# Four batches through an attention, FFN, quaternion attention and expert chain: later turns, spreading in four steps, later loads, and score matmuls in pairs of half the rows

## Time and profile before

| what | us |
|---|---|
| median of 3 runs | 871.47 (870.83 to 872.36) |
| the profiled execution | 872.1 |
| its span | 869.9 |
| TensorE busy in the span | 736.0 (85%) |
| ScalarE busy | 501.3 (58%) |
| VectorE busy | 419.1 (48%) |
| GpSimd busy | 180.4 (21%) |

### The profile page before, as it was taken

One profiled execution on the slowest core, in us unless ns is written; L12 is line 12 of the kernel. 1 busy time (PEld: TensorE's weight loads), 2 busy tenths in 40 slices (PEclk: granted clock), 3 DMA queues, 4 the chain that ended last, 5 costly groups with the idle time before them and its releaser, 6 DMA issues. The chain is left out here.

```text
span 869.9 us, 21028 instructions
## 1 busy us (share of the span) xinstructions
PE 736.0 (85%) x8160; PEld 522.1 (60%) x8160; DVE 419.1 (48%) x1389; ACT 501.3 (58%) x1030; POOL 180.4 (21%) x307
## 2 busy tenths in 40 slices
PE   4779997989779999888989987887786878789994
PEld 3668775768545667665555753455553656467763
DVE  3355426664253464225353566473866646531236
ACT  3456564586557586866658765558454556543231
POOL 7101010000100000010100005132315287036230
PEclk9999998999889999999999999999887999989997
DMA  4610400002400000511000412000511021101010
GB/s 113 204 15 3 152 7 5 5 2 64 126 4 14 17 2 15 149 29 17 4 15 1 127 46 72 19 22 22 165 46 43 26 80 37 33 26 50 19 40 24
DMA packets 72358, 40.43 MB, mean 46 GB/s; under 512 B 42726, under 2 KB 62140, under 8 KB 72132
## 3 DMA queue, kind: packets, MB, share of 16 engines
q1 hardware_dynamic: 70468, 35.81, 15.1%
q0 software_dynamic: 1536, 3.15, 1.2%
q10 hardware_dynamic: 256, 0.13, 0.1%
HBM read 20.98 MB, written 17.96 MB: 45 GB/s over the span
## 5 line engine op out<-in xcount | busy, mean ns | idle before, releaser
L954 ACT ACTIVATE late<-ps,j_bias 128x512 f32<-128x512 f32 x256 | 173.9, 695 | 136.3 <-PE ps L1768 135.4
L1220 DVE TENSOR_REDUCE neg_max<-ps 128x2 f32<-128x32 f32 (+31 forms) x128 | 90.5, 707 | 188.3 <-PE ps L1612 179.7
L1768 PE MATMUL ps<-q_heads,k_parts 128*128 128x512 f32 x256 | 131.6, 531 | 20.8 <-ACT late L954 17.2
L794 ACT ACTIVATE probsT<-ps 128x128 f32<-128x128 f32 (+3 forms) x271 | 102.8, 429 | 76.7 <-PE ps L1627 50.0
L880 ACT ACTIVATE probs<-ps,neg_max 128x16 f32<-128x16 f32 (+31 forms) x256 | 110.5, 494 | 16.7 <-DVE neg_max L1220 16.3
L1627 PE MATMUL ps<-ident,probs 128*128 128x128 f32 x640 | 97.1, 283 | 7.5 <-ACT probs L880 7.5
L664 POOL TENSOR_TENSOR q_wide<-qT,eighth_mask 128x1024 f32<-128x1024 f32 x16 | 31.3, 1954 | 303.2 <-PE ps L1612 175.9
L1627 PEld LDWEIGHTS ps<-ident,probs 128*128 128x128 f32 x640 | 76.8, 144 | 26.7 <-ACT probs L880 10.7
L1768 PEld LDWEIGHTS ps<-q_heads,k_parts 128*128 128x128 f32 x256 | 48.5, 197 | 68.9 <-ACT late L954 46.7
L1783 PE MATMUL ps<-late,v_two 128*9 128x512 f32 x512 | 71.3, 630 | 10.9 <-DVE late L1206 8.7
L1605 PE MATMUL ps<-kT_two,q_wide 64*64 64x262 f32 (+16 forms) x1024 | 74.8, 357 | 4.4 <-ACT probsT L794 2.7
(11 more groups left out here) (271 smaller groups left out, 1166.3 us busy)
## 6 DMA issues: line engine op xcount, KB each, us to landing
k_parts<-k_half SPq DMA_DIRECT2D x16, 256.0 KB, 3.1
q_parts<-q_half SPq DMA_DIRECT2D x16, 256.0 KB, 3.9
k_parts<-k_parts SPq DMA_DIRECT2D x16, 256.0 KB, 3.3
q_heads<-q_parts SPq DMA_DIRECT2D x64, 64.0 KB, 2.2
x_by_expert<-q_heads SPq DMA_DIRECT2D x3, 960.0 KB, 7.7
probsT<-x_by_expert SPq DMA_DIRECT2D x45, 64.0 KB, 1.9
y_by_expert<-probsT SPq DMA_DIRECT2D x45, 64.0 KB, 1.5
q_rel<-q_by_token SPq DMA_DIRECT2D x128, 8.0 KB, 2.4
```

The costliest lines, as they stand in the source:

```text
L794: return nc.scalar.activation(o, i, ACT.Copy)
L954: nc.scalar.activation(head_probs[:, i % SLOTS, :], ps[:, banks[i % len(banks)], :], ACT.Exp, bias=j_bias[:]).then_inc(e2_ready.sem, 1)
L1220: nc.vector.tensor_reduce(neg_max[:, n % 4, :], ps[:, k:k + OCT, 0:QS * (n + 1)], axis=AXX, op=ALU.max, negate=True).then_inc(max_ready.se ...
L1768: mm(ps[:, banks[i % R], :], k_parts[:, hg, kc * P:(kc + 1) * P], q_heads[:, hg % 2, g, :], start=True, stop=True).then_inc(s2_ready.sem, 1)
```

## The change

- The turn of F (pieces 5 and 6) stands three slots later in rounds 1 to 3; in round 4 all F pieces from 5 on stand three slots later (the last twelve one).
- In round 5 N's pieces from 7 on stand three slots later, and its last six later still. In round 4 N's pieces of batch 1 begin one slot later.
- X of batch 0 begins in slot 33 in place of 30.
- S is four pieces: stores; waits and the first group's loads; two loads of k; the rest. They stand in slots 52, 55, 58 and 63 (53, 56, 59 and 63 in round 4).
- The loads of x for batches 1 to 3 are issued behind the expert weights' loads.
- In batches 2 and 3, Q issues two heads' scores in every even step, each over 64 rows (heads 0 and 2, then 1 and 3), into the two banks, after all earlier exps; odd steps issue no scores. The order of heads in a group becomes 0, 2, 1, 3 there, and `values` takes its exps by that order.

```diff
--- before.py
+++ after.py
@@ -93,31 +93,33 @@
             put(r, 0, "A", a - 1, 6)
             put(r, 6, "N", q - 1, 2)
             if a < B:
-                put(r, 6 + late, "F", f, 7)
+                put(r, 6 + late, "F", f, 5)
+                put(r, 14 + late, "F", f, 2)
                 put(r, 17 + late, "F", f, 17)
                 put(r, 34 + late, "F", f, 1)
                 put(r, 38 + late, "F", f, 12)
             else:
                 put(r, 8, "F", f, 5)
-                put(r, 16, "F", f, 20)
-                put(r, 39, "F", f, 12)
+                put(r, 19, "F", f, 20)
+                put(r, 40, "F", f, 12)
             if a == 0:
                 put(r, 1, "W", 0, 46)
             if a + 1 < B:
                 put(r, 41, "H", a + 1, 2)
                 put(r, 47, "H", a + 1, 10)
                 put(r, 52, "R", a + 1, 1)
-            put(r, 52, "S", f, 1)
-            put(r, SL - 1, "S", f, 1)
+            for slot in (52, 55, 58, SL - 1) if a < B else (53, 56, 59, SL - 1):
+                put(r, slot, "S", f, 1)
             if q - 1 == 0:
                 put(r, 52, "N", 0, 20)
             if q - 1 == 1:
-                put(r, 51, "N", 1, 5)
+                put(r, 52, "N", 1, 5)
                 put(r, 59, "N", 1, 15)
-                put(r, 30, "X", 0, NX, 2)
+                put(r, 33, "X", 0, NX, 2)
             if q - 1 == 2:
                 put(r, 10, "N", 2, 5)
-                put(r, 18, "N", 2, 15)
+                put(r, 21, "N", 2, 9)
+                put(r, 32, "N", 2, 6)
                 put(r, 17, "X", 1, NX, 2)
                 put(r, 33, "C", 0, 4, 3)
                 put(r, 50, "C", 0, 4)
@@ -449,6 +451,11 @@
         def quat_banks(b):
             return [QS_BANK] if b + 2 < B else [QS_BANK, 0]
 
+        def heads_in_turn(b):
+
+
+            return [0, 1, 2, 3] if len(quat_banks(b)) == 1 else [0, 2, 1, 3]
+
         block = ctx.enter_context(nc.Block())
 
         @block.sync
@@ -466,8 +473,6 @@
             for m, w in enumerate(QBIAS):
                 sp.dma_start(qbias_in[:, m, :, :], w.rearrange("(a w) o -> a w o", a=1)).then_inc(ld_rows, 16)
             sp.dma_start(q_bias_rep[:], bq.rearrange("(a e) -> a e", a=1).broadcast_to([P, P])).then_inc(ld_bias, 16)
-            for b in range(1, B):
-                sp.dma_start(x_all[:, b, :, :], X[b].rearrange("(t p) e -> p t e", p=P)).then_inc(ld_x, 16)
             sp.dma_start(wi_in[:, 0, :].rearrange("p (f d) -> p f d", f=FT),
                          w_gate.rearrange("(f p) d -> p f d", p=P)).then_inc(ld_ffn, 16)
             sp.dma_start(wi_in[:, 1, :].rearrange("p (f d) -> p f d", f=FT),
@@ -515,6 +520,8 @@
             def weights(b):
                 sp.dma_start(w1_in, w1.rearrange("(m p) e d -> p m e d", p=P)).then_inc(ld_experts, 16)
                 sp.dma_start(w2_in[:], w2).then_inc(ld_experts, 16)
+                for b in range(1, B):
+                    sp.dma_start(x_all[:, b, :, :], X[b].rearrange("(t p) e -> p t e", p=P)).then_inc(ld_x, 16)
                 yield
                 yield
                 for m, w in enumerate(MATS):
@@ -544,10 +551,12 @@
                 sp.wait_ge(q_half_ready.sem, q_half_ready.at(b, 1))
                 for c in range(4):
                     sp.dma_start(q_dram[b][:, c, :, :], q_half[:, c % 2, :].bitcast(f32)).then_inc(q_out.sem, 16)
+                yield
                 sp.wait_ge(k_out.sem, k_out.at(b + 1, 0))
                 sp.wait_ge(q_out.sem, q_out.at(b + 1, 0))
                 spread_k(b, 0)
                 spread_q(b, 0)
+                yield
                 spread_k(b, 1)
                 spread_k(b, 2)
                 yield
@@ -1758,8 +1767,18 @@
                     pe.wait_ge(pT_first.sem, pT_first.at(B, 0))
                     pe.wait_ge(pT_second.sem, pT_second.at(B, 0))
                 for i in range(NCH + 5):
-                    hg, kc, g = i // (KC * GH), i // GH % KC, i % GH
-                    if i < NCH:
+                    hg, kc, g = i // (KC * GH), i // GH % KC, heads_in_turn(b)[i % GH]
+                    if i < NCH and R > 1:
+                        if i % (KC * GH) == 0:
+                            pe.wait_ge(k_spread[hg].sem, k_spread[hg].at(b + 1, 0))
+                            pe.wait_ge(q_spread[hg].sem, q_spread[hg].at(b + 1, 0))
+                        if i % 2 == 0:
+                            pe.wait_ge(e2_ready.sem, e2_ready.at(b, i))
+                            for half, head in enumerate(heads_in_turn(b)[i % GH:i % GH + 2]):
+                                rows = slice(64 * half, 64 * half + 64)
+                                mm(ps[:, banks[half], :], k_parts[rows, hg, kc * P:(kc + 1) * P],
+                                   q_heads[rows, hg % 2, head, :], start=True, stop=True).then_inc(s2_ready.sem, 1)
+                    elif i < NCH:
                         if i % (KC * GH) == 0:
                             pe.wait_ge(k_spread[hg].sem, k_spread[hg].at(b + 1, 0))
                             pe.wait_ge(q_spread[hg].sem, q_spread[hg].at(b + 1, 0))
@@ -1781,7 +1800,8 @@
                     pe.wait_ge(attn2_ready.sem, attn2_ready.at(b, hg))
                 for g in range(GH):
                     last = mm(ps[32 * g:32 * g + D + 1, QV, :], v2_two[:, b % 2, kc, hg * GH + g, :],
-                              head_probs[:, (GH * j + g) % SLOTS, :], start=(kc == 0), stop=(kc == KC - 1))
+                              head_probs[:, (GH * j + heads_in_turn(b).index(g)) % SLOTS, :],
+                              start=(kc == 0), stop=(kc == KC - 1))
                 last.then_inc(av2_ps.sem, 1)
 
             def norm(b):
```

## The result

| | before | after |
|---|---|---|
| median, us (same chip) | 871.51 (870.83 to 872.36, 4 runs) | 890.61 (889.32 to 893.78, 4 runs) |
| ratio | | 1.0224 [1.0195, 1.0253] |
| profiled execution, its span | 872.1, 869.9 | 890.14, 887.9 |
| mean granted TensorE clock | 0.947 | 0.923 |

The account below looks back on a forecast made before the run. It took TensorE's instruction list as the bound, its idle time as the possible gain. Terms -7.7 - 5.4 - 1.0 + 4.0 + 4.7 = -5.4 us took 872.1 to 866.7 profiled, median 866.1, stated as 866; range 856 to 877.

Parts of the forecast that it names:

- turns of rounds 1 to 3, and spreading: Rounds 1 to 3: later turns fill TensorE's holes, 1.0, 2.5 and 0.7 us; round 4: spreading ends a DMA wait, 5.4.
- round 4: F's turn, expert tiles: Round 4: the later turn gains 2.5 of a 3.2 us hole, batch 1's later expert tiles 1.0 more.
- round 5: batch 2's norm: Round 5: the last norm's turn three slots later gains 1.0 of a 4.2 us hole.
- loads of x: Start of the kernel: loads moved behind the weights delay SyncE's chain, costing 4.0 us, between 1.5 and 5.6.
- pairs: Batches 2 and 3, 64 pairs of scores: cost 4.7 us in sum, bounds -4 and +14.
- The thin pair's 1.9 us: Pairs where turns hold little else: 1.9 us round trip for 1.63, 0.27 more each, 3.2 us for twelve.
- if both halves run at once one stream is saved: About 35 crowded pairs: some 0.25 us saved against 0.34 for two tiling changes; +0.02 each taken, 0.7 in all.
- my 0.17 us: Idle time of a 64-row weight load behind 128-row transposes, taken as the cost of one tiling change.
- My first rival: Rounds 4 and 5: crowded pairs pay 0.35 us each for tiling, 12.3 for 35; median 876.9; chance 0.2.
- Second rival, the holes come back: VectorE is the wall behind each turn, so holes only change their name; median 872.8 us; chance 0.17.
- The third rival: Loads cost only their issuing, +1.5 us, and the holes close, turns 11; median 856.6; chance 0.15.
- if TensorE's idle time before L1627 and L1783 grows: Sign of a wrong forecast: TensorE's idle time grows before these lines by what L1484 loses, as the second rival says.

Follow-up runs that it names:

- e10: Kernel before with F's turn three slots later in rounds 1 to 3 and the spreading in four steps, nothing else: 867.26 us, ratio 0.9917.
- g3: The same kernel as e10, run again beside the kernel before on a third chip: 868.79 us, ratio 0.9957.
- f3: e10 plus all of the change's round 4 moves (F's turn, batch 1's norm and expert tiles later): ratio 0.9970 to the kernel before.
- e7: Kernel before with only batch 2's norm in round 5 moved as in the change, first nine pieces and last six: ratio 1.0085.
- f4: Kernel before with only the loads of x moved behind the two weight loads: 876.72 us, ratio 1.0034.
- f2: Kernel before with only the pairs over 64 rows, the same program as e2 on another chip: ratio 1.0110.
- e8: Kernel before with only the last six pieces of batch 2's norm in round 5 moved, slot 27 to 32: ratio 1.0060.
- e9: Kernel before with the pairs alone, but each score over all 128 rows: ratio 1.0025.
- g2: e10 with batch 1's norm one slot and its expert tiles three slots later in round 4, F's turn unmoved: ratio 1.0063 to the kernel before.
- e2: Kernel before with only the pairs over 64 rows, no turn, load or spread moved: ratio 1.0083.
- r_before: The kernel before, unchanged, profiled again on another chip: 875.75 us in one profile.

## Why the prediction was wrong, step by step

| part | forecast, us | measured, us |
|---|---|---|
| turns of rounds 1 to 3, and spreading | -4.2 - 5.4 | -7.2 and -3.7 (e10, g3) |
| round 4: F's turn, expert tiles | -2.5 - 1.0 | +4.6 and +1.1 (f3, -2.6, less either) |
| round 5: batch 2's norm | -1.0 | +7.4 (e7) |
| loads of x | +4.0 | +3.0 (f4) |
| pairs | +4.7 | +9.6 (f2) |
| sum | -5.4 | +17.4 |

The measured parts, each by its own ratio times 872, add up to nearly what the change cost (19.1). Each has an interval of 2 to 3 us on either side, and round 4 is the difference of runs on two chips, so that the sum comes so near is in part luck.

*Round 5's norm: the step that failed most, 8.4 us.* I wrote "In round 5 the slots that come in front hold expert tiles, which need a copy from VectorE: 1.0 of 4.2" and priced the turn alone. The change also moves N's last six pieces from slots 27 to 32 to slots 32 to 37, and the sums' gathers begin in slot 33. I never followed those pieces to GpSimd, whose scatters they hold. Whatever the phase of the rest, the six traces with this move have a hole of 4.6 to 6.4 us at that expert tile, the fourteen without it 2.1 to 2.6; e8 shows it with the turn left alone. In after TensorE then runs at its lower clock (0.50 of full speed from 724 to 734 us). Not all of the 7.4 us need be the scatters': e7's hole at the turn also grew, from 4.2 to 7.8 us, and how much of that is mere phase no run separates.

*Pairs, 4.9 us.* The thin pair's 1.9 us was right where the clock held (e9: 1.85), and so was the smallness of the round trip as a whole (2.2). But only the last four pairs are thin in this way: before's last eight steps take 6.5 us and e9's 7.4, which is all that e9's last stretch is longer by, not the 3.2 us of twelve pairs. That f2's is 3.2 longer is luck: 2.9 of it stands in the same eight steps, at the lower clock. Of the 64 pairs the sum also priced only 12 and 35. The failed step is "if both halves run at once one stream is saved [...] but the array changes its tiling twice": both accounts are in instructions' durations, and the cost came with the granted clock, which slows the instructions around the pairs. The Trainium skill (TensorEngine Tiling (Array Packing), Key Properties) says that a change of the mode drains TensorE; f2 against e9 shows that this is not what counts here. Nor was my 0.17 us a measure of it: in after's trace the weight loads of 64-row scores behind 128-row ones stand idle for 0.12 us in the median, those between two 128x128 ones, with no change of tiling, for 0.14 (of the loads with any idle time). My first rival had the right place and sign, its size in the crowded pairs is refuted: 12.3 us for 35 of them against 0.4 to 1.1 for 20.

*Round 4, 4.6 to 8.1 us.* F's turn did what I said where it stands: the hole of 3.2 us goes in f3's trace, and the stretch up to exp 24 is 4.2 us shorter. What is left of that at the end of the round is not shown. But where I wrote "for the shorter hole at their beginning I take 1.0 more", the tiles' holes grew from 5.2 us (g3) to 9.6 (g2): the first tile now waits for its rows (DMA), and the next holes are VectorE's. Why the rows come late was not tried.

*Turns and spreading in rounds 1 to 4:* the mechanism was right, the sum too large (-9.6 for -3.7 to -7.2). The turns won 4.3 us before round 4 for 4.2, by the means above, and the hole of 4.68 us on the DMA went. But a wait of 2.20 remains there, and the later part of round 4 is 2.9 us shorter (e10, 86.3 for 89.2) where I had 5.4.

*Second rival, the holes come back:* true of the changed kernel's round 5 (L1493's waits fell from 22.4 to 5.8, those of L1656, L1647 in before, rose from 5.3 to 13.3), false in rounds 2 and 4, where TensorE has no wait left before L1493 (260.51 and 543.01 us in after).

*Loads:* right, within the interval (1.1 to 4.8 us for 4.0). x's loads took 13.1 us from issue to landing for 4.1, and the gap of 1.67 us at 62.18 is found again near 67:

```profile
67.04 0.41 PE L1611 MATMUL ps<-kT_far_two,q_wide 64*64 64x2 f32 x8 [3.43 <-DMA q_rel<-q_by_token]
```

The third rival falls by the time itself; its 1.5 us for the loads lies in the interval too. Of my signs, "if TensorE's idle time before L1627 and L1783 grows" named the wrong lines; it grew before L1647.

## What to carry to other kernels

When a group of pieces is moved, list what each of them issues on every engine, GpSimd's indirect transfers first, and lay that beside what the new slots already hold there; the piece that is meant (the turn) may be the cheap one. Where matmuls over half of the rows replace full ones, their neighbours are to be priced at the lower level of the clock as well: in the last stretch of batch 3's scores all seven traces with them lost the full clock, none of the thirteen others did. And every hole of TensorE of some microseconds is to be counted with the slow matmuls that follow it.

## What the runs showed of the hardware that was not expected

**A small VectorE instruction held until GpSimd's copies end.** The 4.72 us above are spent on 128x4 elements; its twin takes 0.17. In 18 such holds of a tensor_scalar (1.5 to 6.1 us) in the kernels' traces, and in five of the scalar_tensor_tensor behind it (5.9 us each, in e9, f3, f4, g2 and g3), the end lies 0.02 to 0.03 us after the end of one of GpSimd's copies for an expert tile, after a burst of up to some 15 instructions without a gap. In e7:

```profile
656.50 6.06 DVE L1084 TENSOR_SCALAR root<-y_moments 128x4 f32<-128x4 f32 x1
```

```profile
661.93 0.60 POOL L737 COPY probsT<-w2T 128x512 f32 x1
```

656.50 + 6.06 = 662.56, 661.93 + 0.60 = 662.53. The Trainium skill (SBUF — State Buffer, Who interferes with whom) says that VectorE and GpSimd share a port pair that one holds for a whole instruction; the trace fits that, but here the one that waits gets on only behind many instructions, and no run shows that the port is the cause. Every one of the 20 traces has such a hold at the turn of round 5. Whether the chain meets the burst at its beginning (6 us) or nearer its end (3 us) is a matter of phase, and the turn's hole goes with it: 6.5 to 7.8 us in the eight traces with a hold of 5.9 or 6.1, 7.0 in after with a hold of 4.7, at most 5.1 in the eleven with a hold of 2.9 to 4.3 (before: a hole of 4.2 with 3.8). By these holes I estimate that a kernel which meets the burst at its beginning loses 2 to 3 us more here than before did. That is read from traces; no run removed the burst.

**VectorE and ScalarE pause while GpSimd issues scatters, on some chips.** In e2, on one of the two chips of the first eight runs, VectorE started nothing for 11.83 us and ScalarE for 14.63, until the last of the eight scatters was out:

```profile
532.20 0.95 POOL L715 DMA_INDIRECT x_by_expert<-xn,row_no  x1 [0.30 <-issue]
```

```profile
534.67 0.69 DVE L1042 COPY outT<-ps 128x512 f32<-128x512 f32 x1 [11.83 <-remote]
```

In r_before, on the other of the two, VectorE's longest such pause was 4.54 us and ended while the scatters went on; the first eight steps of batch 2's scores took 18.96 us there for 11.56 in before, the same program. On the other chips the same scatters ran beside all engines. What waits for what there stays open.
